# Transformer on one Trainium2 core: paired masks in the triangular inverse, a decay column by transposes, waits and turns in another order

## The reference

```python
# layer 2, per chunk
A0 = tril(-(k_beta @ k.T * L), -1)
A = solve_triangular(eye - A0, eye, lower=True, unit_diagonal=True)
# layer 3, per row t
alpha = sigmoid(x @ Wa.T + ba)
beta = sigmoid(x @ Wb.T + bb)
Sk = S @ k_t
S = alpha * (S - beta * outer(Sk, k_t)) + beta * outer(v_t, k_t)
o = q_t @ S
```

## Time and profile before

| | |
|---|---|
| median of 3 runs | 1735.27 us (1735.03 to 1737.14) |
| profiled execution, span from first to last instruction | 1734.0 us |
| TensorE (PE) busy | 1698.0 us |
| its weight loads (PEld) busy | 1300.6 us |
| VectorE (DVE) busy | 1234.6 us |
| GpSimd (POOL) busy | 1218.5 us |
| ScalarE (ACT) busy | 1088.9 us |

### The profile page before, as it was taken

The page is one execution under the profiler, slowest core; times in us unless marked ns, Lnnn a source line. Parts: engine busy times, 40 slices in busy tenths (PEclk is TensorE's granted clock), DMA queues, the critical chain, the costliest instruction groups (busy, mean ns, idle before and its releaser), DMA issues.

```text
span 1734.0 us, 31744 instructions
## 1 busy us (share of the span) xinstructions
PE 1698.0 (98%) x10006; PEld 1300.6 (75%) x10006; DVE 1234.6 (71%) x4490; ACT 1088.9 (63%) x2904; POOL 1218.5 (70%) x1771
## 2 busy tenths in 40 slices
PE   8999999999999999999999999999999899999998
PEld 5788888876667676676666677767788787788976
DVE  7864335688987988988899866445566766578773
ACT  6555226556677678777776786446546666665656
POOL 5655649898878987888789785135347876666667
PEclk9999999999999999999999999999999999999999
DMA  7100000010000000000000000000000001000002
GB/s 254 71 29 1 1 2 3 3 51 1 1 1 1 1 1 1 1 1 1 1 1 1 1 11 6 1 1 7 2 3 3 1 18 31 21 1 2 2 2 73
DMA packets 24027, 26.70 MB, mean 15 GB/s; under 512 B 3492, under 2 KB 20772, under 8 KB 23476
## 3 DMA queue, kind: packets, MB, share of 16 engines
q1 hardware_dynamic: 23860, 24.67, 4.4%
HBM read 22.52 MB, written 2.15 MB: 14 GB/s over the span
## 4 chain that ended last, share of the span: by engine, by line
PE 80%; POOL 6%; DVE 6%; ACT 4%; issue 2%; DMA 0%; SPq 0%; POOLq 0%; ACTq 0%; DVEq 0%
PE ps L87 74%; PE ps L90 7%; POOL arena L104 6%; ACT arena L98 4%; DVE arena L104 2%; DVE arena L110 1%; DVE arena L130 1%; DVE arena L147 1%; ACT arena L99 0%; DVE arena L133 0%; ACT L98 0%; DVE arena L107 0%; DMA arena<-in_x 0%; DVE arena L136 0%; DVE ps L147 0%
## 5 line engine op out<-in xcount | busy, mean ns | idle before, releaser
L104 POOL TENSOR_TENSOR arena<-arena 128x512 f32<-128x512 f32 (+6 forms) x836 | 715.5, 869 | 278.4 <-DVE arena L110 96.9
L98 ACT ACTIVATE arena<-ps 128x128 f32<-128x128 f32 (+11 forms) x1204 | 338.6, 326 | 394.1 <-PE ps L87 287.8
L87 PE MATMUL ps<-arena 128*128 128x128 f32 (+4 forms) x2792 | 441.0, 291 | 10.0 <-DVE arena L104 3.5
L87 PEld LDWEIGHTS ps<-arena 128*128 128x128 f32 x2792 | 373.3, 191 | 97.9 <-issue 46.5
L104 DVE TENSOR_TENSOR arena<-ps,arena 128x128 f32<-128x128 f32 (+4 forms) x696 | 312.9, 468 | 176.0 <-PE ps L87 163.6
L98 ACT ACTIVATE arena<-arena 128x128 f32<-128x128 f32 (+1 forms) x836 | 321.2, 439 | 51.3 <-POOL arena L104 39.6
L87 PE MATMUL ps<-arena,moe 128*128 128x256 f32 (+1 forms) x960 | 288.2, 439 | 0.0
L87 PE MATMUL ps<-arena,cst 128*128 128x504 f32 (+2 forms) x768 | 283.6, 489 | 2.2 <-ACT arena L98 1.1
L98 ACT ACTIVATE arena<-ps,cols 128x512 f32<-128x512 f32 x324 | 216.8, 688 | 103.3 <-PE ps L87 96.5
L104 POOL TENSOR_TENSOR arena<-arena,cst 128x144 f32<-128x144 f32 (+7 forms) x536 | 186.2, 356 | 93.0 <-ACT arena L98 57.4
L110 DVE SCALAR_TENSOR_TENSOR arena<-ps,arena 128x128 f32<-128x128 f32 (+1 forms) x476 | 156.6, 364 | 120.4 <-PE ps L87 94.2
(11 more groups left out here) (120 smaller groups left out, 1756.5 us busy)
## 6 DMA issues: line engine op xcount, KB each, us to landing
rows<-in_rows SPq DMA_DIRECT2D x1, 2253.0 KB, 14.2
arena<-in_x SPq DMA_DIRECT2D x8, 256.0 KB, 5.3
wf<-in_wf SPq DMA_DIRECT2D x2, 1024.0 KB, 6.6
arena<-in_L_ffn_W SPq DMA_DIRECT2D x8, 256.0 KB, 2.9
out_dram<-arena SPq DMA_DIRECT2D x8, 256.0 KB, 2.7
wmod<-in_wmod SPq DMA_DIRECT2D x4, 384.0 KB, 7.7
arena<-kept SPq DMA_DIRECT2D x24, 64.0 KB, 2.9
arena<-kept SPq DMA_DIRECT2D x8, 192.0 KB, 3.0
```

The source lines that it names most:

```text
L87: return UNSENT if self.e is None else self.e.matmul(out, lhsT, rhs, start=start, stop=stop)
L98: return self.e.activation(out, in_, func, bias=bias, scale=scale)
L104: return UNSENT if self.e is None else self.e.tensor_tensor(out, a, c, op)
```

## The change

It has five parts.

1. The inverse's two masked copies of levels 1 to 4 become one GpSimd operation per half, with a four-dimensional pattern that writes both places (`RX`); the two copies of level 0 become one. Levels 5 and 6 stay as they were. For this G4 and X4 of a tile lie next to each other, 320 columns per tile.
2. Layer 3's alpha weight becomes the 258th column of the joined weight. ScalarE makes the sigmoid of one column per tile (al), TensorE spreads the four columns by four transposes of a broadcast column (e3a), and VectorE's eight scans read them from PSUM, after all four tiles' products.
3. The buffers of layer 3 move accordingly (above, gate, qg, u, uT, kd0).
4. Waits ahead of an instruction stand in another order; on TensorE the wait for a free bank now mostly comes last.
5. All four strings of `TURNS` are other ones.

```diff
@@ class Delta
-        G, self.XT, self.Y = r.take(1024), r.take(512), r.take(512)
-        self.G4, self.X4 = G[:, 0:768].rearrange("p (c n) -> p c n", n=192), four(self.XT)
-        self.M4 = self.G4[:, :, 0:128]
+        G, self.Y = r.take(1536), r.take(512)
+        slots = G[:, 0:1280].rearrange("p (c n) -> p c n", n=320)
+        self.M4, self.G4, self.X4 = slots[:, :, 0:128], slots[:, :, 0:192], slots[:, :, 192:320]
+        self.RX = slots[:, :, 128:256].rearrange("p c (k n) -> p k c n", n=64)
@@ inv_pool
+                both = cst[:, ODD:ODD + 14].rearrange("p (k n) -> p k n", n=7)[:, :, n:n + 1].unsqueeze(3)
                 if n == 0:
-                    pool.cp(m.G4[:, :, 128:129], odd).then_inc(*pool.up(b))
+                    pool.cp(m.RX[:, :, :, 0:1], both.broadcast_to([128, 2, 4, 1])).then_inc(*pool.up(b))
...
-                    pool.cp(m.X4[:, :, 0:1], even).then_inc(*pool.up(b))
...
+                elif n < 5:
                     for h in range(2):
+                        x = m.X4[:, 2 * h:2 * h + 2, 0:w].unsqueeze(1).broadcast_to([128, 2, 2, w])
+                        pool.wait_ge(*at("inv_c", b, n - 1, h, *key))
+                        pool.wait_ge(*at("inv_k", b, n - 1, h, *key))
+                        pool.tt(m.RX[:, :, 2 * h:2 * h + 2, 0:w], x, both.broadcast_to([128, 2, 2, w]),
+                                ALU.mult).then_inc(*pool.up(b, "inv_r", b, n, h, *key))
@@ inv_pe, an example of the waits
+                    pe.wait_ge(*at("inv_r", b, n, h, *key))
+                    pe.wait_ge(*at("inv_y", b, n, h, *key))
+                    pe.wait_ge(*at("inv_v", b, n, h, *key))
                     ps = banks.take(pe, b, b, "inv_p", n, h, *key)
-                    pe.wait_ge(*at("inv_v", b, n, h, *key))
-                    pe.wait_ge(*at("inv_y", b, n, h, *key))
-                    pe.wait_ge(*at("inv_r", b, n, h, *key))
@@ l3_pe
-                ps = banks.take(pe, b, b, "e3a", g)
-                pe.mm(ps[:, :], wsm("wa3").broadcast_to([128, 128]), m.hT).then_inc(*pe.up(b, "e3a", b, g))
-                yield
                 for i in range(4):
                     yield
                     ps = banks.take(pe, b, b, "e3k", g, i)
-                    pe.mm(ps[:, 0:257], m.hT[:, col4(i)], wsm("wkvb3")).then_inc(*pe.up(b, "e3k", b, g, i))
+                    pe.mm(ps[:, 0:258], m.hT[:, col4(i)], wsm("wkvba3")).then_inc(*pe.up(b, "e3k", b, g, i))
                 yield
+                ps = banks.take(pe, b, b, "e3a", g)
+                pe.wait_ge(*at("e3al", b, g))
+                for i in range(4):
+                    ins = pe.tr(ps[:, col4(i)], m.al[:, i:i + 1].broadcast_to([128, 128]), ident)
+                ins.then_inc(*pe.up(b, "e3a", b, g))
+                yield
@@ l3_act
-                ps = banks.get(b, "e3a", g)
-                act.wait_ge(*at("e3a", b, g))
-                act.act(m.arow, ps[:, :], ACT.Sigmoid, bias=row("ba3", 0, 1)).then_inc(
-                    *act.up(b, "e3arow", b, g, free=(b, "e3a", g)))
-                yield
...
+                    act.act(m.al[:, i:i + 1], ps[:, 257:258], ACT.Sigmoid, bias=row("ba3", 0, 1)).then_inc(
+                        *act.up(b, "e3al", b, g))
@@ l3_dve
-                    yield
-                    dve.wait_ge(*at("e3arow", b, g))
-                    dve.scan(m.DT[:, c], m.arow[:, c], ident, 0.0, ALU.mult, ALU.add).then_inc(*dve.up(b))
-                    dve.scan(m.grow[:, c], m.arow[:, c], m.arow[:, c], 1.0, ALU.mult, ALU.bypass).then_inc(
-                        *dve.up(b, "e3scan", b, g))
+                ps = banks.get(b, "e3a", g)
+                for i in range(4):
+                    yield
+                    c = col4(i)
+                    dve.wait_ge(*at("e3a", b, g))
+                    dve.scan(m.DT[:, c], ps[:, c], ident, 0.0, ALU.mult, ALU.add).then_inc(*dve.up(b))
+                    dve.scan(m.grow[:, c], ps[:, c], ident, 1.0, ALU.mult, ALU.bypass).then_inc(
+                        *dve.up(b, "e3scan", b, g, free=(b, "e3a", g) if i == 3 else None))
@@ TURNS, the first row of each string for "pe"
-    "pe": ("2000000000000120002230001222000112200011100211012003013211003031110332001332322330320113213131222121"
+    "pe": ("0000030020000020001220002212000121210100102031011200103110001313103023203332122013332111231233121212"
...
```

More of the change, by code:

```diff
@@ L985, in moe0_pe @@
                 yield
-                ps = banks.take(pe, b, b, "m2", g)
                 if g == 0:
@@ L989, in moe0_pe @@
                 pe.wait_ge(*at("mgated", b, g))
+                ps = banks.take(pe, b, b, "m2", g)
                 for i in range(2):
@@ L1459, in project_pe @@
                 pe.wait_ge(*at("l1h", b, l, 0, t // 4))
+            ps = banks.take(pe, b, b, "l1qkv", l, t)
             if l == 0:
```

356 lines of the change are left out of this document (180 added, 176 removed).

## The result

The changed kernel takes **1742.95 us** (median of 4 runs, 1742.37 to 1743.83) against 1735.44 for the kernel before beside it (1735.03 to 1737.14): ratio 1.0038, 95% interval 1.0026 to 1.0050. It is slower, by 7.5 us; the forecast was 1727 and the range ended at 1738.

What follows compares the result with a forecast made beforehand. TensorE was taken to bound the kernel, busy 1698.0 of 1734.0 us. Terms of -3.4 (columns), -3.0 (masks), +1.0 (longer start), 0 (waits) and -3.0 (turns) made -8.4, from 1735.3 to 1727 us; range 1715 to 1738.

Steps and rivals of the forecast that it cites:

- Turns: New queue order: fewer TensorE rows wait directly behind their own element, cutting its idle 36.0 us; -3.0 us.
- The first rival: Only TensorE's columns count; POOL's relief ends in TensorE's queue and the new order gives it back: no difference, chance 0.20.
- POOL's masks: Merged mask operations relieve POOL where it is full, 1340 to 1400 us; half of 6.2 us comes out, -3.0 us.
- Columns: Layer 3's eight group starts: TensorE loses one 512-column matmul and gains four transposes each, all of it counted; -3.4 us.
- Longer start: Layer 3 groups start some 2.9 us longer, mostly covered by other elements' work; +1.0 us, bounds 0 and +11.6.
- The second rival: Eight scans in a row block VectorE in layer 3; half of the 23 us shows: 1743.5 us, chance 0.13.
- Waits: Reordered waits ahead of instructions only change which wait is an instruction of its own; 0 us, bounds -3 and +3.
- The clock rival: At layer 3's group starts transposes replace a long product and TensorE's clock falls: +24 us, 1756 us, chance 0.02.

Runs made afterwards that it cites:

- turns_early: The kernel before with the change's new turns for about the first 1000 us, old turns after, old waits, masks and alpha: 1.0061 of before, +10.4 us.
- masks_waits: The kernel before with the merged masks and the new order of the waits, old turns and old alpha: 1.0006 of before.
- turns_400: The kernel before with the new turns for about the first 400 us only, old turns after: 1.0028 of before, +4.6 us.
- double_scans: The changed kernel with old turns for its first 1000 us and each pair of layer 3 scans run twice: 1.0201 of the kernel before.
- masks_only: The kernel before with the merged masks alone, old waits and old turns: 1.0004 of before.
- w_only: The kernel before with only the change's order of the waits, on all engines; old masks, alpha and turns: 0.9993 of before.
- new_turns_layer2_only: The kernel before with merged masks, new waits, and new turns in layer 2's attention alone, old alpha: 0.9974 of before, 1732.64 us.

## Why the prediction was wrong

- **Turns, -3.0 (bounds -10 and +5).** This is the step that failed: "rows that wait directly behind their own element fall from 736 to 595, by 19%", and idle time with them. Measured: +10.4 us for the turns of layers 0 and 1 in the old kernel (turns_early), +8 in the changed one, beyond my bound. The late turns win in layer 2, but not enough: the changed kernel stands 5.6 us above masks_waits (1.0038 against 1.0006), from which it differs in the turns and the alpha column. The count was right and says nothing of the sign. A row that waits behind its own element costs nothing if the wait is met in time, and 141 rows spread among other elements' rows can meet GpSimd later, as at 299 us in turns_400. The idle 36.0 us that I shared out were the wrong stock as well: the gaps between starts were 145 us.
- **The first rival had the reason** ("an order found for one set of costs need not suit another"), but let it take back the savings and no more. I gave the side of slower to two mechanisms, scans and clock, and none to the order itself, which has the largest reach of all parts.
- **POOL's masks, -3.0 (bounds -6.2 and 0).** The durations held. Groups of GpSimd by shape in after:

```profile
L104 POOL TENSOR_TENSOR arena<-arena,cst 128x64 f32<-128x64 f32 x96 | 27.9, 296 | 23.9 <-ACT arena L98 21.3
L104 POOL TENSOR_TENSOR arena<-arena,cst 128x32 f32<-128x32 f32 x32 | 7.7, 245 | 18.3 <-ACT arena L98 18.3
L104 POOL TENSOR_TENSOR arena<-arena,cst 128x16 f32<-128x16 f32 x32 | 7.0, 224 | 14.6 <-ACT arena L98 14.2
L104 POOL TENSOR_TENSOR arena<-arena,cst 128x8 f32<-128x8 f32 x32 | 6.4, 204 | 18.9 <-ACT arena L98 18.6
L113 POOL COPY arena<-cst 128x8 f32<-128x8 f32 x16 | 4.4, 273 | 0.0
```

  Each merged multiply takes what the row of its own, doubled width took before, and 28.3 us of busy time went. That is 196 ns for each of the 144 instructions. What they are worth is no number of the masks: 0 with the old turns, 7.8 us with the new late ones. In the changed kernel layer 2 wins about 3 us. That is the number that I gave the masks, but by luck: it takes masks and late turns together.
- **Columns, -3.4 whole.** TensorE's stream did get 3.3 us shorter. Layer 3 returned none of it; the transposes taken out again returned about half of their columns, by one trace.
- **Longer start, +1.0 (bounds 0 and +11.6).** By one trace each: right for the chain (0.2) and in size for the scans (0.5 us for 8 us of them); too low for ScalarE's sigmoids, 1.3 instead of nothing. The second rival's price, 11.6, was not paid. Its mechanism shows at twice the scans.
- **Waits, 0 (bounds -3 and +3).** Right with the old turns (0.9993); worth 2.4 to 4.3 us with the new ones.
- **The clock rival.** It did not come: 1.00 at 1340 to 1400 and 1440 to 1640 us, with transposes 9% of the chain from 1340 to 1400 us. The Trainium skill's "TensorE: Matmul & The Clock Gate", Part 4, says that transposes do not count as PE-busy for the clock gate in the same way. The rival that I built on it was priced at 1756, and with this share of transposes the trace shows nothing of it. Where the clock did fall, in double_scans, TensorE was idle for 24 of 200 us.

Summed by the table, the changed kernel is: turns and waits in layers 0 and 1 +6.5, layer 2 -3, layer 3 +2.6. The first is shown by runs from both sides, down to the turns; why these turns are late is shown for one stretch of them, and the cause within layer 3 stays open.

## What to carry to other kernels

The order in which elements are woven into the queues is part of the kernel: price it as a term of its own, with a range as wide as its reach and both signs. A saving on an engine that nobody waits for can be worth nothing under one order and several us under another, so measure the saving with both orders. Splice orders by stage: here the new order in layer 2 alone, with the masks and waits, was worth 3.6 us, and the whole new order cost 7.5. Read the starts of the bound engine's rows, not its busy share, and compare when the same work ends, stage by stage, before any theory. Look at the granted clock of the same stretches, too: a fall in one of the two executions can pass for a loss of the kernel.

## What the runs showed of the hardware

- A delay on the bound engine was carried through unchanged. turns_400 is 3.9 us behind from 400 to 1400 us within 0.1 us, masks_only -0.7 from 50 to 1200. Two executions of nearly the same program agree that closely over a thousand us.
- TensorE's clock at the start differs from one kernel's profiled execution to the next. From 10 to 20 us it was 0.70 before, 0.56 after (above), and w_only had no drop:

```profile
10.00:20.00 10.00, 6.64 (x32) 4.06 (x33) 8.80 (x54) 9.37 (x20) 6.66 (x11) 1.00 0.59 128
```

  This moves everything behind it by up to 2 us (first column of the table: w_only is 2.0 us ahead at 50 us). Its median was 1 us under before, not 3, so single profiled executions of such kernels shouldn't be compared closer than 2 us by their spans. Executions of one kernel differ by it as well: of w_only's eleven, the three with a mean granted clock of 1.000 took 1732.87 to 1734.30 us and the eight with 0.996 to 0.998 took 1735.05 to 1736.47.
- The clock also fell late in some kernels and not in others: its mean from 1680 to 1700 us was 0.91 in masks_only and 1.00 before (both above), and 0.91 in new_turns_layer2_only too, whose gain of 3.1 us at 1650 us is 1.5 at 1700 us.
- VectorE was busy 72% of layer 3's stretch. 26.5 us of scans added there cost about 23 us, and 10 more by TensorE's clock; 8 us taken from it gave 0.5.
- A narrow fp32 pass saved nothing: before, the next start came 0.11 us after 120 of the 152 passes of 8 columns, as it did after most passes of 128.
